# One graph-attention layer with a mixture of experts: another order of the feed-forward part

## What is computed

```python
# graph attention; h_target gives the queries, the normalised x the keys and values
hs, ht = layer_norm(layernorm(x)), layer_norm(h_target)
logits = where(adj != 0, (ht @ Wq + bq) / sqrt(32) @ (hs @ Wk + bk).T, -1e30)   # per head
ht = ht + (softmax(logits) @ (hs @ Wv + bv)) @ Wo + bo
ht = layer_norm(ht)                         # ln2
x  = x + ht + gelu(ht @ W1) @ W2            # feed-forward 256 -> 1024 -> 256
# experts
xn = layernorm(x)
top 2 of xn @ gate_w.T, softmax over the two -> comb
x  = x + sum_e comb[:, e] * (gelu(xn @ w1[e].T + b1[e]) @ w2[e].T + b2[e])
```

## Time and profile before

| what | us |
|---|---|
| median of 3 runs | 1150.33 |
| lowest, highest | 1147.48, 1150.34 |
| the profiled execution, its time | 1153.37 |
| its span in the profile | 1151.6 |
| TensorE busy | 998.4 |
| ScalarE busy | 767.6 |
| VectorE busy | 690.9 |
| GpSimd busy | 584.1 |

### The profile page before, as it was taken

One profiled execution on the slowest core, in us unless ns is written; L12 is line 12 of the kernel. 1 busy time (PEld: TensorE's weight loads), 2 busy tenths in 40 slices (PEclk: granted clock), 3 DMA queues, 4 the chain that ended last, 5 costly groups with the idle time before them and its releaser, 6 DMA issues. The chain is left out here.

```text
span 1151.6 us, 22515 instructions
## 1 busy us (share of the span) xinstructions
PE 998.4 (87%) x7088; PEld 617.3 (54%) x7089; DVE 690.9 (60%) x1987; ACT 767.6 (67%) x971; POOL 584.1 (51%) x477
## 2 busy tenths in 40 slices
PE   3943599999999999999999987989409999999994
PEld 2721244444444444444444544557308888888883
DVE  7825777697778877787777636545423443433432
ACT  4522399889999999999999846542206555555552
POOL 7503488877877777787567742003541323223232
PEclk9975599999999999999999989998659999999997
DMA  6597645565448544563663257515421233233233
GB/s 192 126 311 269 195 162 171 205 211 182 147 128 281 185 139 150 202 245 122 201 211 103 99 204 312 203 31 182 164 82 39 50 45 56 41 53 53 41 56 91
DMA packets 76178, 171.09 MB, mean 149 GB/s; under 512 B 13634, under 2 KB 45250, under 8 KB 70402
## 3 DMA queue, kind: packets, MB, share of 16 engines
q1 hardware_dynamic: 50962, 99.80, 26.3%
q0 software_dynamic: 21280, 69.11, 20.9%
q10 hardware_dynamic: 3856, 1.19, 0.4%
HBM read 123.05 MB, written 63.14 MB: 162 GB/s over the span
## 5 line engine op out<-in xcount | busy, mean ns | idle before, releaser
L1016 DVE CUSTOM_DVE_ANT_0 masked<-ps,maskA 128x512 f32<-128x512 f32 x512 | 346.7, 689 | 112.9 <-PE ps L1433 109.8
L1433 PE MATMUL ps<-ks,qs 96*128 96x512 f32 x512 | 259.9, 547 | 48.9 <-DMA qs<-q_low 24.6
L1320 ACT ACTIVATE masked<-masked,negmax 128x2048 f32<-128x2048 f32 x128 | 256.3, 2003 | 64.1 <-DVE negmax L1022 63.9
L1381 ACT ACTIVATE weights<-ps 128x1024 f32<-128x1024 f32 x256 | 253.5, 1013 | 32.1 <-PE ps L1456 29.7
L1454 PE MATMUL ps<-qs,ks 98*128 98x512 f32 x512 | 228.8, 506 | 2.7 <-DMA qs<-shift_lo 2.5
L1456 PE MATMUL ps<-maskB,identb 128*128 128x512 bf16 x512 | 201.3, 393 | 0.0
L1698 POOL DMA_INDIRECT sum_rows<-y,ids x48 | 74.4, 1551 | 205.6 <-issue 119.2
L1433 PEld LDWEIGHTS ps<-ks,qs 96*128 96x128 f32 x512 | 101.7, 199 | 135.9 <-DVE piecemax L1016 96.5
L1716 DVE TENSOR_TENSOR gT<-ffn_w,gT 128x2048 f16<-128x2048 f32 x25 | 57.3, 2292 | 149.5 <-ACT gT L1766 149.5
L1468 PE MATMUL ps<-weights,v_all 128*32 128x256 f32 x2048 | 137.0, 385 | 0.9 <-ACT weights L1381 0.9
L1797 PE MATMUL ps<-xT,wall 128*128 128x256 f16 x1200 | 136.7, 275 | 0.0
(11 more groups left out here) (182 smaller groups left out, 1152.5 us busy)
## 6 DMA issues: line engine op xcount, KB each, us to landing
expert_rows<-pad_rows POOLq DMA_DIRECT2D x73, 272.0 KB, 6.0
split_weights<-whl POOLq DMA_DIRECT2D x36, 512.0 KB, 3.1
adjA<-in_adj SPq DMA_DIRECT2D x16, 1024.0 KB, 7.9
adjB<-in_adjT SPq DMA_DIRECT2D x32, 512.0 KB, 6.6
wall<-split_weights SPq DMA_DIRECT2D x16, 1024.0 KB, 15.3
wch<-in_w1T POOLq DMA_DIRECT2D x16, 512.0 KB, 6.0
wch<-in_w2T POOLq DMA_DIRECT2D x16, 512.0 KB, 6.2
xr<-expert_rows SPq DMA_DIRECT2D x26, 272.0 KB, 2.7
```

The source lines that it names most:

```text
L1016: dve.tensor_tensor_reduce(masked[:, a % 2, k * 512:(k + 1) * 512], ps[:, u % 2, :], maskA[:, a, k * 512:(k + 1) * 512], 1.0, NO_EDGE, ALU ...
L1320: act.activation(masked[:, a % 2, :], masked[:, a % 2, :], ACT.Exp, bias=negmax[:, h % 2, a:a + 1], accum_out=rowsum[:, h % 4, a:a + 1]).t ...
L1381: act.activation(weights[:, j % 4, :, :], ps[:, 2 + 2 * (j % 2):4 + 2 * (j % 2), :], ACT.Exp).then_inc(weights_ready, 1)
L1433: pe.matmul(ps[:, u % 2, :], qs[0:KR, h % 4, a * P:(a + 1) * P], ks[0:KR, h, k * 512:(k + 1) * 512], start=True, stop=True)\
```

## The change

Only calls are moved; nothing is added or left out, and all waits inside the functions stay as they are.

- SyncE, step n = 30: `load_context(2)` with its wait for attn_ready goes ahead of the load of `ffn_w`.
- VectorE: `scale_shift(2)` goes from behind `attention_moments(3)` to behind `attention_sum(3)`, in the f loop of block 0; `scale_shift(3)` from the middle of block 1's splits to between `ffn_sum(0, 0)` and `ffn_sum(0, 1)`; `split_turned(2)` and `(3)` go ahead of the `ffn_sum` calls.
- ScalarE: `normalise_h(3)` goes from f = 0 to 3 of block 1 to f = 4 to 7; `high_turned(3)` goes ahead of `normalise_x(0)`.
- TensorE: `turn_h2(2)` goes ahead of `back(0, *)`, `turn_h2(3)` ahead of `back(1, 0)`; `ranks(0)` goes from behind f = 4 of block 3's first layer to behind `back(2, 0)`.

```diff
@@ sync, step n = N - 2 @@
                         sp.wait_ge(whl_out, 16 * 4)
-                        load_set(sp, ffn_w, 0, ffn_in)
                         sp.wait_ge(attn_ready, 2)
                         load_context(2)
+                        load_set(sp, ffn_w, 0, ffn_in)
@@ vector @@
                     elif f == 5:
                         attention_sum(3)
+                        scale_shift(2)
                 attention_moments(3)
-                scale_shift(2)
                 dve.wait_ge(c3_ready, 8)
                 dve.tensor_copy(place[:, :], region0[:, :]).then_inc(rank_read, 1)
                 for f in range(FC):
                     split_hidden(1, f)
-                    if f == 3:
-                        scale_shift(3)
+                split_turned(2)
                 ffn_sum(0, 0)
+                scale_shift(3)
                 ffn_sum(0, 1)
-                split_turned(2)
...
+                split_turned(3)
                 ffn_sum(1, 0)
                 ffn_sum(1, 1)
-                split_turned(3)
@@ scalar @@
                 for f in range(FC):
                     hidden_high(1, f)
-                    if f < TPB:
-                        normalise_h(3, (f,))
+                    if f >= FC - TPB:
+                        normalise_h(3, (f - FC + TPB,))
                 high_turned(2)
                 for f in range(FC):
                     hidden_high(2, f)
+                high_turned(3)
                 normalise_x(0)
                 copy_xnT(0)
-                high_turned(3)
@@ tensor @@
                 for f in range(FC):
                     hidden(1, f)
+                turn_h2(2)
                 back(0, 0)
                 back(0, 1)
-                turn_h2(2)
                 for f in range(FC):
                     hidden(2, f)
+                turn_h2(3)
                 back(1, 0)
                 turn_xn(0)
                 back(1, 1)
                 pe.wait_ge(gw_in, 16)
                 gates(0)
-                turn_h2(3)
                 for f in range(FC):
                     hidden(3, f)
-                    if f == 4:
-                        pe.wait_ge(c3_ready, 8)
-                        ranks(0)
                 back(2, 0)
+                pe.wait_ge(c3_ready, 8)
+                ranks(0)
                 turn_xn(1)
```

## The result

| | median us | lowest to highest | runs |
|---|---|---|---|
| before | 1150.34 | 1147.48 to 1154.31 | 4 |
| after | 1137.82 | 1137.38 to 1138.24 | 4 |

The ratio is 0.9889, with a 95% interval of 0.9859 to 0.9919: about 12.8 us faster. Forecast were 16.3 us and 1134.0 us, with 1129.5 to 1141 as the range. The profiled execution of after took 1138.16 us, its span 1136.4; against that of before it is 15.2 us shorter. So the profiled pair moved by nearly what was forecast, the medians by less. That difference is the subject of most of what follows.

A forecast was written before the change was run, and what follows sets the result against it. The wait chain was nearly all TensorE's untouched expert stage; ahead of it, the end of back(2,1) set all that follows. Terms 6.4 + 0.4 + 4.9 + 4.6 = 16.3 us off 1150.3 gave 1134.0 us, 80% range 1129.5 to 1141.

The forecast's parts named there:

- Rival E: Behind back(2,1): scatters or last weights bound elsewhere give back half of Part 3 and part 4; 1138.8 us, chance 0.05.
- Part 1: Third output projection, context loaded ahead of the weights: 3.89 us stall and 2.55 us slow clock gone, 6.4 us gained.
- Rival B: Third output projection: context still late beside POOL's stores and fills, gaining 1.3 instead of 6.4 us; 1139.1 us, chance 0.07.
- Part 2: Block 1's first layer, with block 3's normalisation and scale_shift(2), (3) moved: 0.4 us gained, bounds -2 and +1.0.
- Part 3: Turnings of blocks 2 and 3 moved ahead: 1.57 and 1.58 us idle and 1.8 us slow clock gone, 4.9 us gained.
- part 4: ranks(0) behind back(2,0): 3.13 us idle and 2.7 us slow clock gone, new 1.4 us pause at turn_xn(1); 4.6 us gained.
- A: Feed-forward order gives less: slow clock behind new pauses, VectorE not keeping up in hidden(3); 11.8 us gained, 1138.5, chance 0.20.
- C: hidden(2) and hidden(3) wait as long for another input; 11.4 us gained, 1138.9 us, chance 0.03.
- D: Slower: after the later rank of block 0, turn_xn(1) waits for place to be read on VectorE; 1153.8 us, chance 0.02.

The follow-up runs named there:

- early_ctx: The kernel after with block 2's context load one step earlier, ahead of store_shift(31): median 1137.41 us, ratio to before 0.9851 (0.9810 to 0.9892).
- no_norm: The kernel after with normalise_h(3), scale_shift(2) and scale_shift(3) back in their old places: 1141.07 us against 1135.54 in the same session, ratio to before 0.9895.

## Why the prediction was right, and what it missed

**The range held, the centre was 3.8 us too low.** 1137.8 (and 1135.5 in the later session) lies in 1129.5 to 1141, and the sign is as said. The gain was 12.8 us, then 15.9 by ratio, and 16.9 by the medians in the last session with the early context; the forecast was 16.3. That two of three come near it is partly luck, as the sum holds a term that is a matter of chance (parts 3 and 4 below).

**What bounds.** Right. Everything up to the end of back(2,1) passed through to the boundary; the last stretch was 0.9 us longer in after than in before, which is within its scatter between executions of one kernel (62.2 to 65.2 for before). Rival E did not come.

**Part 1, 6.4 us.** Right in sum, 5.9 us by ratio and 6.0 between quiet profiles. Wrong in the transfer's length: I took the 4.4 us row as nearest, since it had nothing big ahead on SyncE. It landed after 7.4 to 9.4 us, near the 8.4 us of POOL's fill in the same crowd. What decided was the traffic beside it, POOL's or the weights behind it on SyncE or both: early_ctx took the load away from all of it, and it landed in 3.6 us. With 8 us to spare it was just in time, or up to 1.1 us late: the sum of part 1 came out although the landing was mis-sized. Rival B's condition, a late context, was met in four of the seven profiles with this order of loads (0.3 to 1.1 us of waiting), against a chance of 0.07, but the lateness cost at most 1.4 us and not 5.1. The rule cited from the Trainium skill, "DMA: Bandwidth & Descriptors", "Queues, rings and completion order", that an engine goes round between the queue rows, fits a landing that is longer in company (7.4 against 3.6 us), but no run here shows the sharing. The estimate made from it was too short: by 405 GB/s, 512 KB take 1.3 us, so half the bandwidth would turn 3.6 us into 4.9 and not 7.4.

**Part 2, 0.4 us.** The mechanism was right: a pause of 3.4 us through VectorE's split (3.5 forecast). The term was too small, 0.8 by no_norm and up to 2.2 against the two other profiles of before, because the first profile of before, and that of no_norm, happened to have a short slow stretch behind the pause (30 matmuls in 7.98 and 8.07 us, against 9.45 and 9.14).

**Part 3, 4.9 us, and part 4, 4.6 us.** The idle times were right: 3.15 us gone, 3.1 gone, 1.5 new where I had 1.4. The step that failed is the slow clock, 1.8 in part 3 and 2.7 in part 4: I read both off one execution and booked them in full, as a property of the kernel. In two further profiles of the kernel before neither was there. Together the parts are worth 65.2 - 59.5 = 5.7 us in such an execution, and 69.3 - 59.5 = 9.8 in one like the first, against 9.5 forecast. What they are worth on average lies between and is open, since the clock of most executions lay under that of the quiet profiles. I had three hints in the first profile. A pause of 1.57 us had no slow clock behind it, which I used only as a chance for a rival. A pause of 1.67 us in front of hidden(0,0), which the prediction does not list among its pauses, had none either; TensorE in the kernel before:

```profile
694.81 2.75 PE L1510 MATMUL ps<-hT,ffn_w 128*128 128x512 f16 x12 [1.67 <-DVE hT L1107]
```

And the profiled execution lay 3.0 us over the median. I carried that 3.0 us through the sum as an offset common to both kernels, when part of it may be the very thing that the change removes.

**The sum again, for a quiet execution.** With the slow clock of parts 3 and 4 left out, part 2 at 2.1 and part 4 at 2.1, it is 6.4 + 2.1 + 3.15 + 2.1 = 13.8 us. Between the quiet profiles it is 29.4 + 36.2 + 65.2 less 23.3 + 34.0 + 59.5, 14.0 us, and between the medians 12.5 us the first time and 14.7 the second. The sum closes on the idle times; the clock adds up to 4.5 us to it in the executions of before that have it.

**Rivals.** A gave the time nearest to the first median (1138.5), but by another way: no slow clock stood behind the new pause, hidden(3) kept pace, and what was missing were slow clocks that were not there to be removed. C, D and E did not come.

## What to carry to other kernels

Before a slow clock, or any cost that hangs on a state, goes into a sum, look whether an equal pause elsewhere in the same trace went without it, and book it at its share and not in full. One or two more profiles of the kernel before, compared stretch by stretch, give that share better than one; and the clock of all executions tells whether the profiled ones are the usual case. In a strictly ordered list, a step moved ahead for a distant reader must not pass one that a near reader waits for: scale_shift(2) and the moments ahead of the splits, with block 3's normalisation among the GELUs, cost 4.0 us that later places gave back. And a transfer's length is that of its surroundings: 3.6, 7.4 and 11.6 us were measured for one and the same load, with nothing beside it, with other traffic beside it, and with 2048 KB ahead of it on its own queue as well.

## What the runs showed of the hardware

The granted clock does not answer to a pause alone. Counted over all fourteen profiles, from the pause in front of the third projection to back(2,1)'s end, TensorE's pauses of 1.5 us and more fall in three groups. Of 33 pauses of 1.5 to 1.7 us (14 at hidden(0), ten at hidden(2) and hidden(3) with the old turnings, 9 at turn_xn(1) with the rank moved) 32 were followed by a clock of 1.00 and one by 0.50. Of the five pauses of 3.1 to 3.2 us for member two were followed by a slow stretch (0.50 and 0.61). Of the 16 of 3.4 us and more (five for the context, seven of 4.2 us and four of 3.4 us in block 1) all were, at a changing length: behind 4.2 us, 30 matmuls took from 7.98 to 9.48 us, where they take 6.6 at full speed. What decides in the middle group I have not found.

The mean granted clock of an execution went with its time: 54 executions of before lay between 0.929 and 0.939, the lowest 24 took 5.1 us more on average than the highest 16. Kernels with nearly equal instructions ahead of it began the same stretch of the attention up to 8 us apart.

In the four profiles of the last session, one of them of the unchanged kernel, TensorE stopped for 0.5 to 0.6 and then 1.0 to 1.1 us in the midst of back(3,0), and VectorE waited 1.1 to 1.9 us in front of reads of PSUM with no releaser on the core. The stretch also holds fetches of instructions (the DMA queues named instruction), but so it does in the kernel after, which has no such stop; the cause is not shown.
